# Two cross-attentions regrouped: halves of the tokens with four heads a step, instead of all tokens with two heads a step

## The reference, cut to what matters

```python
q = (hidden_states @ Wq).reshape(B, Sq, H, D)            # 16 heads of 128 columns
k = (encoder_hidden_states @ Wk).reshape(B, Skv, H, D)
v = (encoder_hidden_states @ Wv).reshape(B, Skv, H, D)
q = rmsnorm(q, gq)                                       # layer 0 only
k = rmsnorm(k, gk)                                       # layer 0 only
scores = jnp.einsum('bqhd,bkhd->bhqk', q, k) * scale
attn = jax.nn.softmax(scores, axis=-1)                   # layer 1: with a mask over the keys
out = jnp.einsum('bhqk,bkhd->bqhd', attn, v)
return out.reshape(B, Sq, H * D) @ Wo
```

## Time and profile before

| what | us |
|---|---|
| median of 3 runs (1078.93 to 1079.61) | 1079.23 |
| the profiled execution, its own time | 1080.59 |
| its span from first to last instruction | 1078.8 |
| PE busy, DVE busy, ACT busy, POOL busy | 934.3, 607.3, 445.1, 256.9 |
| cross-attention of layer 0, steps and way out (321.5 to 597.6) | 276.1 |
| cross-attention of layer 1, steps (839.7 to 989.9) | 150.2 |

### The profile page before, as it was taken

How to read it: one execution, slowest core, us unless ns; L and a number is a source line. 1 busy time by engine, 2 the same in 40 slices (tenths; PEclk the granted TensorE clock), 3 DMA queues, 4 the chain that set the end, 5 groups by cost and what they waited for, 6 DMA issues and landing times.

```text
span 1078.8 us, 13122 instructions
## 1 busy us (share of the span) xinstructions
PE 934.3 (87%) x5455; PEld 587.3 (54%) x5458; DVE 607.3 (56%) x736; ACT 445.1 (41%) x665; POOL 256.9 (24%) x117
## 2 busy tenths in 40 slices
PE   6778888676799999999998999978978899999755
PEld 3223333222374565676667666655877577777423
DVE  3999899999652322333325444463854344345574
ACT  3744556442216656555452211123334332222376
POOL 0277686867400000000000000010004991000000
PEclk9699898989999999999999899989558999999788
DMA  8555454554541000000000500020000000000001
GB/s 288 137 142 158 123 156 137 155 136 131 199 167 50 1 1 0 2 1 2 1 1 1 228 1 1 1 117 1 3 2 0 1 1 1 1 1 2 0 5 35
DMA packets 17018, 64.43 MB, mean 60 GB/s; under 512 B 2848, under 2 KB 4512, under 8 KB 15456
## 3 DMA queue, kind: packets, MB, share of 16 engines
q1 hardware_dynamic: 16960, 63.60, 19.4%
HBM read 60.05 MB, written 3.15 MB: 59 GB/s over the span
## 4 chain that ended last, share of the span: by engine, by line
PE 63%; DVE 24%; ACT 9%; issue 3%; DMA 0%; POOL 0%; DVEq 0%; ACTq 0%
PE ps L854 10%; PE ps L920 10%; DVE region_c L1233 9%; DVE ps L1228 6%; PE ps L963 5%; PE ps L973 5%; PE ps L910 4%; PE ps L888 3%; PE ps L772 3%; PE ps L872 3%; PE ps L726 3%; PE ps L868 2%; ACT region_c L589 2%; PE ps L861 2%; PE ps L836 2%
## 5 line engine op out<-in xcount | busy, mean ns | idle before, releaser
L355 POOL TENSOR_TENSOR region_c<-region_c,region_b 128x1024 f32<-128x1024 f32 x43 | 105.1, 2445 | 84.0 <-DVE region_c L1233 59.8
L920 PE MATMUL ps<-region_c 128*128 128x256 f32 x512 | 117.3, 384 | 2.7 <-ACT region_c L589 2.7
L920 PEld LDWEIGHTS ps<-region_c 128*128 128x128 f32 x512 | 98.2, 193 | 27.4 <-issue 11.5
L367 POOL TENSOR_TENSOR x<-x,region_a 128x2048 f32<-128x2048 f32 x1 | 4.5, 4524 | 436.1 <-DVE xn L1143 436.1
L1233 DVE TENSOR_TENSOR_SCAN region_c<-region_c,ps 128x1024 f32<-128x1024 f32 x43 | 98.3, 2286 | 1.5
L772 PE MATMUL ps<-region_c,ident 128*128 128x512 f32 x172 | 88.3, 638 | 6.7 <-DVE region_c L1212 6.0
L1295 DVE TENSOR_TENSOR region_c<-region_c 128x512 f32<-128x512 f32 x32 | 22.1, 692 | 119.8 <-ACT region_c L564 119.8
L1228 DVE TENSOR_TENSOR ps<-ps,region_c 128x1024 f32<-128x1024 f32 x64 | 78.9, 1232 | 9.9 <-PE ps L760 4.8
L760 PE MATMUL ps<-region_b,sel_b 96*128 96x512 bf16 x128 | 41.8, 410 | 48.6 <-DVE ps L1228 48.4
L589 ACT ACTIVATE region_c<-ps 128x512 f32<-128x512 f32 x64 | 36.9, 597 | 106.2 <-PE ps L910 106.2
L760 PEld LDWEIGHTS ps<-region_b,sel_b 96*128 96x128 bf16 x128 | 9.8, 101 | 99.4 <-DVE ps L1228 87.7
(11 more groups left out here) (208 smaller groups left out, 1676.8 us busy)
## 6 DMA issues: line engine op xcount, KB each, us to landing
region_b<-m_rows SPq DMA_DIRECT2D x43, 512.0 KB, 4.5
region_c<-m_rows SPq DMA_DIRECT2D x21, 512.0 KB, 4.4
region_a<-in_x_wo SPq DMA_DIRECT2D x2, 2048.0 KB, 11.7
m_rows<-region_b SPq DMA_DIRECT2D x4, 512.0 KB, 5.6
region_a<-in_x_wq SPq DMA_DIRECT2D x1, 2048.0 KB, 9.3
region_b<-in_f_fc SPq DMA_DIRECT2D x1, 2048.0 KB, 7.6
region_b<-in_f_proj SPq DMA_DIRECT2D x1, 2048.0 KB, 12.0
region_a<-in_x_wqT SPq DMA_DIRECT2D x1, 2048.0 KB, 14.9
```

Source lines behind the costliest of these rows:

```text
L355: pool.tensor_tensor(m_hc[u % 3], m_h[u % 3], m_cb[u % 3], ALU.mult).then_inc(sem("m_hc"), 1)
L920: last = pe.matmul(tiles2(t // 2)[:, t % 2, :], o_T[:, a, 128 * t:128 * t + 128], wvo[:, 2 * i + a, :], start=(i == 0 and a == 0 and t % 2 ...
```

## The change

In both cross-attentions the eight steps `it` are now 2 halves of the tokens by 4 groups of heads: a step takes 512 tokens (`cols(it)`) and four heads. Queries, keys, turned probabilities, contexts and output sums are as many products as before over a step, or the same columns in fewer products; the order within a step is: for each head a of four `queries`, `keys`, `project_out(it - 2, a)` of one row tile over four heads.

In layer 0 the norms change too. The keys are kept without their norms, and the gains `g_col` go into the queries' copy. The sums of squared keys, `key_squares`, are computed after all four heads as products with 64 output rows each: even batches on output rows 0 to 63, odd ones on 64 to 127, 256 columns each. The reciprocal roots `k_rn` are then multiplied into the scores, a second multiplication in `shift`. The sums of squared queries are computed as rows, `query_squares`: four products with 32 output rows each and 512 columns, head a on output rows 32a to 32a + 31. ScalarE copies them to `q_rows`, and `query_norms` turns them into columns with four products by `head_rows`, a constant with one 1 for each head. `scores(it)` waits for less of VectorE's work. The exponentials stand behind the second head's queries.

In layer 1 only the grouping changes; the mask stands once, and is read again for each head. The first two banks of the output sums are complete four steps earlier than the others.

```diff
--- before.py
+++ after.py
...
+        head_rows = small[:, 44:48]
...
-        k_gain = view("C", 16, [TOK])
-        k_sq = view("C", 20, [TOK])
-        k_rn = view("C", 24, [TOK])
-        k_T = [view("C", 28 + 4 * i, [TOK]) for i in range(2)]
-        q_sq = view("C", 36, [TOK])
+        k_sq = view("C", 16, [4, HALF])
+        q_sq = view("C", 24, [4, HALF])
+        k_T = view("C", 32, [4, HALF])
+        k_rn = [view("A", 24 + 4 * i, [4, S * 4]) for i in range(2)]
+        q_rows = view("A", 32, [HALF])
...
-            for i in range(NH // 2 + 1):
-                if i < NH // 2:
...
+            for it in range(8 + 1):
+                if it < 8:
+                    for a in range(4):
+                        order += [(("q", it, a), "act")]
                         if layer == 0:
-                            order += [(("k", 2 * i + a, c), "act") for c in range(2)]
-                            order += [(("ss", 2 * i + a, c), "act") for c in range(2)]
-                            order += [(("qn", 2 * i + a, 0), "act")]
-                if i >= 1:
-                    order += [(("pT", i - 1, a), "dve") for a in range(2)]
-                    order += [(("o", i - 1, n), "act") for n in range(4)]
+                            order += [(("k", it, a), "act")]
+                    if layer == 0:
+                        order += [(("ss", it, 0), "act"), (("ss", it, 1), "act"), (("qr", it, 0), "act")]
+                if it >= 1:
+                    order += [(("pT", it - 1, c), "dve") for c in range(2)]
+                if it < 8 and layer == 0:
+                    order += [(("qn", it, 0), "act")]
+                if it >= 1:
+                    order += [(("o", it - 1, n), "act") for n in range(4)]
...
-                def queries(h):
+                def queries(it, a):
+                    b = bank(("q", it, a))
+                    if layer == 0:
+                        act.activation(q_sq[:, a, :], b, ACT.Square)
+                        act.activation(q_T[:, a, :], b, ACT.Copy, scale=g_col).then_inc(freed, 1)
+                    else:
+                        act.activation(q_T[:, a, :], b, ACT.Copy).then_inc(freed, 1)
+
+                def keys(it, a):
+                    b = bank(("k", it, a))
+                    act.activation(k_sq[:, a, :], b, ACT.Square)
+                    act.activation(k_T[:, a, :], b, ACT.Copy).then_inc(freed, 1)
+
+                def key_norms(it):
                     for c in range(2):
...
+                        b = bank(("ss", it, c))
+                        if c == 0 and it >= 2:
+                            act.wait_ge(sem("x0_t"), it - 1)
+                        rn = k_rn[it % 2][:, 2 * c:2 * c + 2, :].rearrange("p a n -> p (a n)")
+                        act.activation(rn, b, ACT.Ln, scale=1.0 / HD, bias=eps_col).then_inc(freed, 1)
+                        act.wait_ge(freed, turns[("ss", it, c)][2])
+                        act.activation(rn, rn, ACT.Exp, scale=-0.5).then_inc(sem("x0_rk"), 1)
+                    act.activation(q_rows, bank(("qr", it, 0)), ACT.Copy).then_inc(freed, 1)
+
+                def query_norms(it):
+                    b = bank(("qn", it, 0))
+                    lnq = small[:, 96:112]
+                    act.activation(lnq, b[:, 0:16], ACT.Ln, scale=1.0 / HD, bias=eps_col).then_inc(freed, 1)
+                    act.wait_ge(freed, turns[("qn", it, 0)][2])
+                    if it >= 1:
+                        act.wait_ge(sem("x0_raw"), it)
+                    act.activation(small[:, 112:128], lnq, ACT.Exp, scale=-0.5).then_inc(sem("x0_rq"), 1)
+
+                for it in range(8 + 1):
+                    for a in range(4):
+                        if it < 8:
+                            queries(it, a)
+                        if it >= 1 and a == 1:
+                            exps(it - 1)
+                        if it < 8 and layer == 0:
+                            keys(it, a)
+                    if it < 8 and layer == 0:
+                        key_norms(it)
+                        query_norms(it)
+                    if it >= 1:
...
-                def queries(h):
+                def cols(it):
+                    return slice(it // 4 * HALF, it // 4 * HALF + HALF)
+
+                def queries(it, a):
+                    h = 4 * (it % 4) + a
+                    b = bank(("q", it, a))
+                    for k in range(KH):
+                        w = wq[:, k, HD * h:HD * h + HD] if layer == 0 else wqk[:, h, k, :]
+                        last = pe.matmul(b, w, xnT[:, k, cols(it)], start=(k == 0), stop=(k == KH - 1))
+                    last.then_inc(filled, 1)
+
+                def keys(it, a):
+                    h = 4 * (it % 4) + a
+                    pe.matmul(bank(("k", it, a)), wk[:, HD * h:HD * h + HD], ctxT[:, cols(it)],
+                              start=True, stop=True).then_inc(filled, 1)
+
+                def key_squares(it):
...
+                        b = bank(("ss", it, c))
+                        pe.wait_ge(sem("x0_free_act"), turns[("k", it, 2 * c + 1)][2])
+                        for a in range(2):
+                            for r in range(2):
+                                sq = k_sq[:, 2 * c + a, :].rearrange("p (j r k) -> p r j k", r=2, k=S)[:, r]
+                                last = pe.matmul(b[64 * r:64 * r + 64, 256 * a:256 * a + 256], ones[:, 0:64], sq,
+                                                 start=True, stop=True)
                         last.then_inc(filled, 1)
...
+                def query_squares(it):
+                    b = bank(("qr", it, 0))
+                    for a in range(4):
+                        last = pe.matmul(b[32 * a:32 * a + 32, :], ones[:, 0:32], q_sq[:, a, :], start=True, stop=True)
+                    last.then_inc(filled, 1)
+
+                def query_norms(it):
+                    b = bank(("qn", it, 0))
+                    pe.wait_ge(sem("x0_free_act"), turns[("qr", it, 0)][2])
+                    for t in range(4):
+                        last = pe.matmul(b[:, t:t + 13:4], q_rows[:, 128 * t:128 * t + 128], head_rows,
                                          start=True, stop=True)
                     last.then_inc(filled, 1)
...
+                def scores(it):
+                    pe.wait_ge(sem(tag + "_free_act"), turns[("q", it, 3)][2])
+                    if it >= 1:
+                        pe.wait_ge(sem("x0_raw" if layer == 0 else "x1_t"), it)
...
+                    if layer == 0:
+                        pe.wait_ge(sem("x0_free_act"), turns[("k", it, 3)][2])
+                    for a in range(4):
+                        keys_T = k_T[:, a, :] if layer == 0 else ctxT[:, cols(it)]
+                        for b in range(B // 2):
+                            c = 256 * (a % 2) + S * (b // 2)
+                            last = pe.matmul(ps[64 * (b % 2):64 * (b % 2) + 64, 4 + a // 2, c:c + S],
+                                             q_T[:, a, S * b:S * b + S], keys_T[:, S * b:S * b + S],
+                                             start=True, stop=True)
                     last.then_inc(sem(tag + "_s"), 1)
 
...
-                def context(i):
...
+                def context(it):
+                    pe.wait_ge(sem(tag + "_free_dve"), turns[("pT", it, 1)][2])
                     for n in range(4):
...
+                        b = bank(("o", it, n)).rearrange("p (s a q) -> p s a q", s=2, a=4)
+                        r, m = n % 2, n // 2
+                        for s in range(2):
+                            mov = p_T[64 * r:64 * r + 64, :, 128 * m + S * s:128 * m + S * s + S]
+                            last = pe.matmul(b[:, s], ctxn[64 * r:64 * r + 64, 4 * (it // 4) + 2 * m + s, :], mov,
                                              start=True, stop=True)
                         last.then_inc(filled, 1)
...
+                def project_out(it, t):
+                    if t == 0:
+                        pe.wait_ge(sem(tag + "_free_act"), turns[("o", it, 3)][2])
+                    for a in range(4):
+                        last = pe.matmul(tiles2(2 * (it // 4) + t // 2)[:, t % 2, :], o_T[:, a, 128 * t:128 * t + 128],
+                                         wvo[:, 4 * (it % 4) + a, :], start=(it % 4 == 0 and a == 0 and t % 2 == 0),
+                                         stop=(it % 4 == 3 and a == 3), skip_group_check=True)
+                    if t % 2 and it % 4 == 3:
+                        last.then_inc(sem(tag + "_out"), 1)
+
+                for it in range(8 + 2):
+                    for a in range(4):
+                        if it < 8:
+                            queries(it, a)
                             if layer == 0:
-                                keys(h)
-                        if i >= 2:
-                            project_out(i - 2, a)
-                        if h < NH and layer == 0:
-                            norms(h)
-                    if 1 <= i <= NH // 2:
```

(52 more changed lines are left out.)

150 lines of the change are left out of this document (29 added, 121 removed).

## The result

The kernel after takes 1039.60 us (median of 4 runs, 1039.09 to 1042.44), the kernel before in the same comparison 1079.08 (4 runs, 1078.02 to 1079.61): a ratio of 0.9641, 95% interval 0.9622 to 0.966, 39.5 us less. The profiled execution took 1039.63 us (before 1080.59), its span is 1037.8, TensorE is busy 884.6 us of it, DVE 595.1, ACT 421.0, at a mean clock of 0.933 (before 0.924).

What follows compares the result with a forecast made beforehand. TensorE was taken to set the pace in layer 0. Layer 0 gives 29.4 - 1.5 - 1.2 = 26.7 us, layer 1's way out 3.3: 30.0 off the 1079.2 median makes 1049, range 1041 to 1059.

Steps and rivals of the forecast that it cites:

- way out of layer 0: End of layer 0, 26.1 us before: early row tiles let VectorE start the last pair at once, 1.2 us less.
- the four strips: `query_squares` in layer 0's steps: four 512-column products on 32 output rows each overlap, taking 0.9 us.
- Bank waits: Layer 0's step tail: two waits on ACT around the transposes, together 1.3 us.
- The first fill step: Layer 0's first step, without output sums and contexts: 23.7 us before, 22.0 without slow clock, forecast 19.9.
- Rivals 2 and 3: Layer 0's strips: (2) one product's instructions don't overlap, 1053, chance 0.14; (3) strips don't overlap, 1071, chance 0.06.
- Rival 3: Layer 0: strips don't overlap at all; step of 32.0 us, stage some 8 us shorter, 1071 in all; chance 0.06.
- Rivals 4 and 5: Layer 0's tails: (4) low clock in all eight, 1056, chance 0.12; (5) half speed through next queries, 1132, chance 0.06.
- rival 4: Low clock comes in every layer 0 step's tail, eight times 1.5 to 2 us: 1056; chance 0.12.
- I take four such stretches instead of three: Layer 0: four stretches near half clock instead of three, each about 1.5 us, so 1.5 us given back.
- changes of shape: TensorE in layer 0: 0.15 us a step for changed product shapes, 1.2 in all; bounds nothing to 3.6.
- C: Theory after the result: the kind of TensorE work decides where its clock falls; the change removed two kinds.
- neither theory: C, or P: only when idle time and work fall counts, and the change or this execution fell well.

Runs made afterwards that it cites:

- one_strip: Kernel after, query sums of all four heads written by the same 32-column tile, norms of heads 1 to 3 uncomputed: 1056.47 us, one run.
- cols_back: Kernel after, sums of squared queries again as 16 one-column products a step, no rows: 1067.07 us, ratio 0.9887.
- l1_only: Kernel before with only layer 1 changed, layer 0 old: 1072.61 us, ratio 0.9933.
- before_shift2: Kernel before with two more 512-column products on TensorE ahead of layer 0's cross-attention: 1080.41 us, ratio 1.001.
- before_one: Kernel before, each head's eight one-column query-sum products cut to one of eight columns, other tokens' norms uncomputed: 1070.36 us, ratio 0.9918.
- l0_only: Kernel before with only layer 0 changed, layer 1 old: 1046.27 us, ratio 0.9705.
- after_shift2: Kernel after with two more 512-column products on TensorE ahead of layer 0's cross-attention: 1043.26 us, ratio 0.9663.
- strip_order: Kernel after, a bank's key sums taken into one tile first, then the other, instead of in turn: 1040.99 us, one run.
- narrow_ctx: Kernel after, each context product split in two of 128 columns, as before: 1046.32 us, ratio 0.9695.
- logs_first: Kernel after, ScalarE's tail reordered: both logarithms, then the copy of the rows, then both key exponentials: 1036.43 us, ratio 0.9605.
- rows_early_shift2: `rows_early` with two more 512-column TensorE products, which ran behind layer 0's cross-attention: 1034.35 us, ratio 0.9573.
- rows_early: Kernel after, queries squared before keys, `query_norms` before transposes, ScalarE copying rows first, key exponentials last: 1034.83 us, ratio 0.957.

## Why the prediction was right in its steps and wrong in its sum

**Right.** Every length of a step: 28.7 forecast, 28.68 measured; way out of layer 0 24.9 (26.1 less 1.2) and 24.8; steps of layer 1 20.6 and 20.5; squared keys 1.95 where 1.7 to 1.9 was said; the four strips 0.99 where 0.9 was. Bank waits of 0.26 and 0.43 us, with the hand-over about 1.0 us, where 1.3 was. The first fill step was 0.5 us longer than reckoned (20.4, not 19.9), the second as reckoned (24.2 and 24.3). Rivals 2 and 3 are refuted by the strips' time, and `one_strip` shows what the four strips' part of 3 would have cost (2.2 us a step, 17 us in one run). Rival 3's "some 8 us shorter" holds only if the six steady steps alone grow by 3.3 us (249.4 + 19.8 = 269.2, 6.9 less than 276.1); with all eight nothing would be left. Rivals 4 and 5 did not come: no step of the profile is below 1.00. But `cols_back` shows rival 4's mechanism in full, some 1.8 us in each of eight tails, with 16 one-column products in a row.

**Wrong: "I take four such stretches instead of three", the term for the clock.** Of layer 0 the forecast left 249.4 us; its own lengths, without clock and shapes, make 19.9 + 24.3 + 6 x 28.7 + 24.9 = 241.3; measured 242.0. The difference of 8.1 is three items: the slow clock of before carried over into the new steps (1.7, 1.4 and 2.1 in steps one, two and eight, and 0.2 of rounding: 5.4), a fourth stretch (1.5), and 1.2 for changes of shape. None came; 0.7 came back from the fill step and step eight (29.2). That is 7.4 us. In layer 1 the clock was no term at all: the forecast started from output sums of 8.95 us and kept them; in the kernel after they take 7.17, and the contexts before them 1.2 less, 3.0 in all, with 0.05 us in each step besides: 3.5 us more than forecast. 7.4 + 3.5 = 10.9, and the profiled executions differ from the forecast by 11.0. The clock is nearly 10 of it (5.4, 1.5 and most of the 3.0). It is also why the range didn't hold: its lower end takes out layer 0's stretches and the changes of shape, and leaves layer 1's output sums at 8.95 us.

Why they did not come: for layer 1's way out this is shown, the narrow contexts are the cause. For layer 0 it stays open. Low stretches in its steps and on its way out, by profile:

| layer 0's work | profile | low stretches |
|---|---|---|
| as before | `before` | steps 1, 2 and 8 |
| as before | `l1_only` | steps 6 and 7, way out |
| as before | `before_shift2` | none |
| query sums cut | `before_one` | way out |
| as after | `after`, `l0_only`, `one_strip` | none |
| as after | `after_shift2`, `strip_order` | step 1 |
| contexts narrow | `narrow_ctx` | none |
| tail reordered | `logs_first`, `rows_early_shift2` | none |
| tail reordered | `rows_early` | way out |

(`one_strip` and `strip_order` have the products of the kernel after with another tile or order.) The old work has more of them in two of three profiles, which speaks for C, but none in the third; the new work has one in three of nine. So neither theory holds alone, and up to the 5.2 us of the three stretches in the profile of before (1.7, 1.4 and 2.1) may be luck of the execution: the forecast took one execution's stretches for a property of the kernel. The other executions point the same way. The kernel before took 1076.93 to 1083.62 us over all comparisons, at mean clocks of 0.930 to 0.918, and one of the four runs of the kernel after took 1042.44 at 0.929, where the others took 1039.09 to 1039.63 at 0.933. No run separates when a stage begins from what else differs between two executions.

**The charge for changes of shape** (1.2, at most 3.6) is near nothing: the steps come out at the length reckoned without it. By the Trainium skill (TensorEngine Tiling (Array Packing), Key Properties) a change of tiling mode drains TensorE. The trace shows no such cost that adds to the sum: a drain may be in the 0.99 us of the four strips, for which the bound was 0.86, or in the bank waits, and more than that doesn't show.

By the Trainium skill (TensorE: Matmul & The Clock Gate, Measured speedup vs the span model) three strips ran 2.38 times as fast as in turn; here, four ran 3.6 times as fast as on one strip (0.99 and 3.55 us).

## What to carry to other kernels

Where a profile has low-clock stretches, forecast them as a term of its own, with both ends: all gone and one in each step; and take more than one profile of the kernel before, because a stretch in one execution may be missing or elsewhere in the next. Here that term was worth nearly 10 of the 11 us of error, while lengths of steady steps worked out instruction by instruction, with the bank each waits for, held within 0.1 us in 28.7. Sums over the partitions for a norm belong in wide products on several tiles, with the result turned back: the one-column products cost TensorE's time, and 16 of them in a row ahead of the scores its clock too. Before shortening a piece of TensorE's work, ask whose work it covers: alone, this one gave 9 us of the 26 expected. And look in the trace where an added piece of work really runs before reading a run by it.

## What the runs showed of the hardware

A row of 16 one-column float32 products (32 instructions) ahead of the scores went with a granted clock of about half, 1.2 of 2.4 GHz, in every step of `cols_back` (window 338 to 345: 0.52), though TensorE was busy all of those 7 us; half as many in a row went without it in all eight steps of `before_shift2`. Contexts of 128 columns and 64 rows on layer 1's way out ran at low clock in five of five profiles, those of 256 columns in none of nine. Other stretches came and went between executions of the same work (`rows_early` and `rows_early_shift2` up to the end of layer 0: 3.0 us on its way out). Four products on four tiles of 32 columns run together in 0.99 us, against 3.55 on one tile.
